# Transposing attention probabilities in 32-row pieces, four row groups into four banks, in a two-layer decoder kernel

## The reference

```python
scores = jnp.einsum('bhqd,bhkd->bhqk', Q, K) * scale
scores = jnp.where(mask == 0, jnp.float32(-1000000000.0), scores)
probs = jax.nn.softmax(scores, axis=-1)
attn = jnp.einsum('bhqk,bhkd->bhqd', probs, V)
```

## Time and profile before

| What | Value |
|---|---|
| Median of 3 runs | 1174.74 us (1174.51 to 1176.31) |
| The profiled execution | 1172.23 us, of which the span of the profile is 1170.4 us |
| Mean granted TensorE clock | 0.936 of full |
| PE / PEld busy | 946.8 us (81%) / 752.5 us (64%) |
| DVE / ACT / POOL busy | 888.7 us (76%) / 509.1 us (43%) / 309.4 us (26%) |
| One tile in the periodic stretch (l1 mixes start at 447.58 and 512.45 us) | 64.9 us |

### The profile page before, as it was taken

One profiled execution on the slowest core, in us unless ns is written; L12 is line 12 of the kernel. 1 busy time (PEld: TensorE's weight loads), 2 busy tenths in 40 slices (PEclk: granted clock), 3 DMA queues, 4 the chain that ended last, 5 costly groups with the idle time before them and its releaser, 6 DMA issues.

```text
span 1170.4 us, 23205 instructions
## 1 busy us (share of the span) xinstructions
PE 946.8 (81%) x8774; PEld 752.5 (64%) x8774; DVE 888.7 (76%) x2135; ACT 509.1 (43%) x1377; POOL 309.4 (26%) x508
## 2 busy tenths in 40 slices
PE   5657778888888888888888888888888888878754
PEld 5444656676676776776767766767666767657633
DVE  3775677888797888788797888878887888777452
ACT  2322436363536355363636354453636263534320
POOL 2561121312222222223222232232222222312121
PEclk9677999999999999999999999999999999989876
DMA  9102000000000000000000000000000000000000
GB/s 338 37 5 73 10 8 15 3 19 8 20 8 15 10 17 10 14 14 3 20 7 15 13 15 11 16 11 3 24 3 20 3 6 8 6 6 6 6 4 5
DMA packets 24414, 24.47 MB, mean 21 GB/s; under 512 B 2305, under 2 KB 22641, under 8 KB 24177
## 3 DMA queue, kind: packets, MB, share of 16 engines
q1 hardware_dynamic: 24304, 22.98, 6.1%
HBM read 18.80 MB, written 2.10 MB: 18 GB/s over the span
## 4 chain that ended last, share of the span: by engine, by line
DVE 47%; PE 30%; ACT 11%; issue 6%; POOL 6%; DMA 0%; DVEq 0%; POOLq 0%; SPq 0%
PE bank L1125 21%; PE bank L1240 9%; DVE peak L918 7%; ACT prob L663 6%; ACT prob L657 3%; DVE ma_ L1037 3%; DVE stats L847 2%; DVE q_top L809 2%; DVE y_ L861 2%; POOL scratch L528 2%; POOL rstd L522 2%; DVE k_ L1061 2%; DVE scratch L905 2%; DVE x_ L873 1%; DVE k_ L1070 1%
## 5 line engine op out<-in xcount | busy, mean ns | idle before, releaser
L663 ACT ACTIVATE prob<-bank,low 128x128 f32<-128x128 f32 x384 | 104.4, 382 | 156.6 <-DVE low L925 156.6
L1240 PE MATMUL bank<-cst,prob 128*128 128x128 f32 x768 | 117.2, 303 | 54.7 <-DVE y_ L861 39.0
L519 POOL TENSOR_TENSOR var_eps<-mean_var,rsq 128x1 f32<-128x1 f32 x144 | 28.4, 198 | 468.3 <-DVE mean_var L850 468.3
L1240 PEld LDWEIGHTS bank<-cst,prob 128*128 128x128 f32 x768 | 96.1, 156 | 71.9 <-issue 62.6
L918 DVE TENSOR_REDUCE peak<-bank 128x4 f32<-128x512 f32 x192 | 126.3, 684 | 20.8 <-PE bank L1125 20.8
L601 ACT ACTIVATE xt_<-bank 128x256 f32<-128x256 f32 x144 | 54.9, 393 | 130.5 <-PE bank L1240 130.3
L601 ACT ACTIVATE probT<-bank 128x512 f32<-128x512 f32 x192 | 103.5, 602 | 17.4 <-PE bank L1240 17.4
L522 POOL TENSOR_TENSOR rstd<-var_eps,rsq 128x1 f32<-128x1 f32 x144 | 79.8, 554 | 11.3
L1125 PE MATMUL bank<-w_gu,xt_ 128*128 128x352 f32 x256 | 81.0, 470 | 1.5 <-ACT w_f L601 1.0
L1125 PE MATMUL bank<-xt_,w 128*128 128x128 f32 x512 | 70.5, 304 | 0.5 <-ACT xt_ L601 0.5
L1125 PEld LDWEIGHTS bank<-xt_,w 128*128 128x128 f32 x512 | 69.4, 221 | 1.2 <-ACT xt_ L601 1.2
(11 more groups left out here) (180 smaller groups left out, 2202.7 us busy)
## 6 DMA issues: line engine op xcount, KB each, us to landing
xtin<-in_xT SPq DMA_DIRECT2D x16, 128.0 KB, 2.3
next_<-in_x SPq DMA_DIRECT2D x16, 128.0 KB, 6.9
ct_<-in_ctxT SPq DMA_DIRECT2D x16, 128.0 KB, 7.7
w<-in_w SPq DMA_DIRECT2D x2, 1024.0 KB, 6.1
out<-x_ SPq DMA_DIRECT2D x16, 128.0 KB, 1.7
next_<-x_ SPq DMA_DIRECT2D x16, 127.0 KB
rowt<-in_rows SPq DMA_DIRECT2D x1, 1664.0 KB, 7.7
w<-in_gate_up SPq DMA_DIRECT2D x2, 512.0 KB, 9.4
```

Of the source, the lines that this page charges most:

```text
L663: ins = act.activation(prob[:, r, c * P:(c + 1) * P], bank[r][:, c * P:(c + 1) * P], ACT.Exp, scale=SCALES[layer], bias=low[:, b, h:h + 1])
L1240: ins = pe.transpose(dst[:, k * P:(k + 1) * P], src[:, k * P:(k + 1) * P], ident)
```

## The change

`mix` now cuts each 128x128 transpose into four pieces of 32 queries. Piece g takes partitions 32g to 32g+31 of `prob` as the stationary operand (32 rows, 128 columns) and the 32x32 corner of the identity as the moving one (32 columns); it uses row group g of the array and writes 32 columns of bank `t{g}`. One mix is 64 such pieces. The bank no longer stands for the head group r but for the queries g, so each of the four banks is full only after the last r. TensorE waits for all four banks ahead of the first piece. ACT's four copies stay as many and as large; `value` reads the moving operand as four runs of 32 columns, 512 apart.

```diff
@@ STAGE_FILLS
-    ... _l + "_mix": [f"t{r}" for r in BANK_ORDER], ...
+    ... _l + "_mix": [f"t{g}" for g in range(4)], ...
@@ mix on ACT
-                    for r in BANK_ORDER:
-                        copy(i, (layer + "_mix", b, f"t{r}"), probT[:, r, :])
+                    for g in range(4):
+                        copy(i, (layer + "_mix", b, f"t{g}"), probT[:, g, :])
@@ mix on TensorE
                 def f(i, b):
+                    keys = [(layer + "_mix", b, f"t{g}") for g in range(4)]
                     for r in BANK_ORDER:
-                        key = (layer + "_mix", b, f"t{r}")
                         if r < 2:
                             pe.wait_ge(exped, at(i, SCORES, layer + "_scores", b, 2, r))
                         else:
                             wait_empty(pe, i, (layer + "_scores", b, S_BANKS[r]))
-                        turn_tile(i, key, prob[:, r, :], 4)
+                        if r == BANK_ORDER[0]:
+                            dsts = [free(i, key) for key in keys]
+                        for c in range(4):
+                            at0 = 32 * (4 * r + c)
+                            for g in range(4):
+                                part = slice(32 * g, 32 * g + 32)
+                                ins = pe.transpose(dsts[g][:, at0:at0 + 32], prob[part, r, c * P:(c + 1) * P],
+                                                   ident[part, part])
+                                if (r, c) == (BANK_ORDER[3], 3):
+                                    filled(ins, keys[g])
@@ weigh, value
-                        ins = mm(..., values[:, 4 * c + r, :], weights[:, r, c * P:(c + 1) * P])
+                        ins = mm(..., values[:, 4 * c + r, :], weights(r, c))
+            def turned(r, c):
+                at0 = 32 * (4 * r + c)
+                return probT[:, :, at0:at0 + 32]
-                    filled(weigh(dst, v_[:, b, :, :], probT), key)
+                    filled(weigh(dst, v_[:, b, :, :], turned), key)
```

More of the change, by code:

```diff
@@ L90 @@
 for _l in ("l0", "l1", "x1"):
-    STAGE_FILLS.update({_l + "_scores": S_BANKS, _l + "_mix": [f"t{r}" for r in BANK_ORDER], _l + "_value": ["y"],
+    STAGE_FILLS.update({_l + "_scores": S_BANKS, _l + "_mix": [f"t{g}" for g in range(4)], _l + "_value": ["y"],
                         _l + "_back": ["yb"], _l + "_turn": ["yt"], _l + "_out": ["o"]})
@@ L1314, in weigh @@
                     for r in range(4):
-                        ins = mm(dst[32 * r:32 * r + 32, c * P:(c + 1) * P], values[:, 4 * c + r, :],
-                                 weights[:, r, c * P:(c + 1) * P])
-                return ins
+                        ins = mm(dst[32 * r:32 * r + 32, c * P:(c + 1) * P], values[:, 4 * c + r, :], weights(r, c))
+                return ins
+            def turned(r, c):
+                at0 = 32 * (4 * r + c)
+                return probT[:, :, at0:at0 + 32]
             def value(layer):
@@ L1441, in l1_ma_value @@
                 dst = free(i, key)
-                filled(weigh(dst, e_[:, b % 2, :, :], ma_), key)
+                filled(weigh(dst, e_[:, b % 2, :, :], lambda r, c: ma_[:, r, c * P:(c + 1) * P]), key)
             def l1_ma_back(i, b):
```

## The result

| | Median, us | Ratio to before, 95% interval | Granted clock | At half clock, us |
|---|---|---|---|---|
| Before | 1175.53 | | 0.936 | 150 |
| Changed | 1269.68 (1267.76 to 1274.33) | 1.0806 (1.0774 to 1.0838) | 0.874 | 319 |

The change costs 94 us, where 41 had been forecast. The sign and the places were right; the time lies outside of the range, whose top was 1254. The last column is worked out as 2 x (1 - granted clock) x span, since the clock stood at one or the other of its two levels, 2.4 and 1.2 GHz, all the time.

A forecast was written before the change was run, and what follows sets the result against it. Bound by a chain of waits between engines through three mixes. 34 us (fifteen periods) + 3 (other mixes) + 4 (clock) = 41 on 1172.23, 1213; the median stands 2.5 higher: 1216 us. Range 1195 to 1235; 8 in 10: 1190 to 1254.

The forecast's parts named there:

- What bounds the kernel: No engine is full; a chain of waits passes through all three mixes of a period, and VectorE passes delays on in full.
- The pieces: In each mix, a round of four pieces takes 0.068 us, set by the load; 16 rounds take 1.09 us at full clock.
- rival 1: Slow loads in the mixes: 0.107 us a round, 75 us in all, 1250 us; chance 0.15.
- The banks: Mixes await four empty banks and hand over only at the end: next stage +0.61 to +0.77 (l0), +0.48 (x1), +1.05 us (l1).
- the terms for the waits and the pieces: Three mixes add 2.2 us a period, 34 us over fifteen periods, plus 3 us for the three mixes outside them.
- The late copies ahead of `l1_value`: Behind the l1 mix, all four copies end at about 516.6 in place of 515.15, delaying `l1_value`; costed at nothing.
- `value`: Its 16 matmuls stay; reading the moving operand in runs of 32 columns costs 0, upper end some 3 us.
- The clock: A few more l0 mixes fall to half clock, 1.7 us each: 4 us, with ends 0 and 12.
- Rival 2: The x1 or l1 mix also goes to half clock, 1.7 us a period: 25 us on top, 1241 us; chance 0.14.

The follow-up runs named there:

- the 64-row pieces: Kernel before, with the last two head groups of each mix transposed in 64-row pieces, two row groups into the two last banks; 1180.4 us.
- fillers ahead and behind: Changed kernel plus matmuls of constants, read by nobody, in TensorE's waits ahead of the pieces (11, 8, 2) and behind them (2, 0, 2); 1205.0 us.
- all its fillers: Kernel before plus matmuls of constants, read by nobody, in TensorE's waits in the mixes and in `x1_turn_h` (8 there); 1151.5 us.
- fillers in the mixes of the kernel before: Kernel before plus matmuls of constants, read by nobody, in TensorE's waits in the l0 and x1 mixes, none in `x1_turn_h`; 1167.5 us.

## Why the prediction was wrong

- *What bounds the kernel*: right. All three mixes were on the chain, and each delay went on in full.
- *The pieces*: right, slightly high. 64 pieces in 1.19 us are (1.19 - 0.22) / 63 x 4 = 0.062 us a round, against 0.068. The row groups load and multiply at once; loads of 32 rows x 128 columns of transposes cost 0.06 a round, not the 0.107 of rival 1. That the load sets this pace is borne out by the 64-row pieces: a round of two took 0.065 us, with twice the moving columns and half the instructions.
- *The banks*: right. From the last piece's start to the next stage 0.95 us in the l1 mix (559.01 to 559.96), against 0.97; the delays 0.66, 0.41 and 0.94 against 0.77, 0.48 and 1.05. With the mixes' waits filled on both sides, changed against before is 1205.0 - 1167.5 = 37.5 us, where the terms for the waits and the pieces were 34 + 3. That it fits so closely is in part luck, as the two weren't at half clock for the same time (127 and 137 us).
- *The late copies ahead of `l1_value`*: a small miss, costed at 0 ("so I add nothing for it"). A period without a fall of the clock shows it, first in the changed kernel with fillers ahead and behind (1205.0 us), then in the kernel before with all its fillers (1151.5 us):

```profile
530.36 0.42 DVE L975 TENSOR_TENSOR scratch<-bank,cst 128x256 f32<-128x256 f32 x1 [1.03 <-PE bank L1127]
...
534.28 1.08 PE L1127 MATMUL bank<-probT,v_ 128*32 128x128 f32 x32 [0.30 <-ACT probT L603]
...
542.28 2.48 DVE L1039 TENSOR_TENSOR ma_<-bank,cst 128x512 f32<-128x512 f32 x4 [0.18 <-PE bank L1127]
...
596.02 0.42 DVE L975 TENSOR_TENSOR scratch<-bank,cst 128x256 f32<-128x256 f32 x1 [1.04 <-PE bank L1127]
```

```profile
506.58 0.42 DVE L974 TENSOR_TENSOR scratch<-bank,cst 128x256 f32<-128x256 f32 x1 [1.04 <-PE bank L1126]
...
517.20 2.48 DVE L1038 TENSOR_TENSOR ma_<-bank,cst 128x512 f32<-128x512 f32 x4
...
569.65 0.42 DVE L974 TENSOR_TENSOR scratch<-bank,cst 128x256 f32<-128x256 f32 x1 [1.03 <-PE bank L1126]
```

  One tile takes 596.02 - 530.36 = 65.66 us and 569.65 - 506.58 = 63.07, so with the clock held the change costs 2.6 us a period. DVE's instructions behind the three mixes are later by 1.03 (l1), 0.81 (l0) and 0.46 us (x1), within 0.04 of the forecast 1.05, 0.77 and 0.48. The remaining 0.27 comes in at `ma_`: TensorE waits 0.30 us for the copies ahead of `l1_value`, and `ma_`, some stages on, now waits for TensorE. That is 4 us in all.
- *`value`* with its operand in runs of 32: the 32 instructions take 1.08 us before and after; costing it at 0 held.
- *The clock*: the step that failed. "I add 4 us for a few more that fall; the ends are 0 and 7 x 1.7 = 12." The fillers in the mixes give back 1269.7 - 1205.0 = 65 us in the changed kernel and 1175 - 1167.5 = 8 before, 57 us net. That 57 + 37.5 makes the 94 measured proves nothing, since the same four times stand in both; but the length of a period gives the same without them. It was 70.65 us on average in the changed kernel (DVE's `x0_project` at 273.27 and, 11 periods on, at 1050.46) and 64.8 before (253.42 and 1031.31, 12 periods), 5.8 more. Of these 2.6 are the banks with the clock held, and the 3.2 left are the clock: 48 us in 15 periods, and the ends beside them. I had limited it to the l0 mix, where the trace of before showed it, and to periods that had not fallen yet; it also fell at the x1 mix, in the waits for the copies and oftener at `x1_turn_h`, nearly three times a period in all. Rival 2 named the mechanism, but for one of the two mixes, at 25 us, and with a chance of 0.14. That one idle stretch of 2.2 of 4 us had stood at 1.00 was weak evidence against it: of two like waits in the l0 mix, the same trace showed one with a fall and one without. The range had no room for it to happen at several places at once. So the step that failed is the size and the reach of the clock term: about 57 us where it had 4, at most 12.

How a fall is tied to the idle time in detail stays open: the same wait of 2.80 us at the l0 mix is followed by half clock within the pieces in some periods, in `w_dn` in others, and why falls at `x1_turn_h`, to which the change does nothing, went from 5 to 10 I haven't settled; the wait there had grown from 2.2 to 3.1 us in seven of the ten. Its length alone isn't the reason: with fillers in the mixes of the kernel before it stayed at 2.2 to 2.3 us, and the falls went from 5 to 12.

## What to carry to other kernels

Splitting a transpose over the row groups does speed it up: 1.19 us here where it had been 1.91. But each row group fills a bank of its own, so no bank is full before the end, and the hand-over to the next engine changes from a pipeline of four to one block; look at when each bank is awaited and released before counting TensorE's own time. Where a change turns several short waits of TensorE into one long wait, price the clock at every such place, and not only where it has fallen before: here that was about 57 of 94 us. Holding the clock at one place can move its falls to the next, as the fillers in the mixes of the kernel before did; look at all places again after each step. Where TensorE waits for others anyway, idle matmuls into a free bank hold its clock, and were worth 2% in the kernel before; more of them cost 5 us again.

## What the runs showed of the hardware

Float32 transposes keep TensorE at full clock like matmuls: 1203.2 and 1205.0 us with either as fillers, both at a granted clock of 0.947. Float32 transposes of 32 rows x 128 columns keep a pace of 0.062 us for four row groups together, 0.0154 us a piece, 64 of them in 1.19 us; those of 64 rows keep 0.065 us for two row groups together, and full ones take 0.11 each. In the one mix that was read, a change from full to 64-row transposes cost 0.09 us (0.20 from start to start in place of 0.11), and the way back to a full matmul 0.04 (0.15 in place of 0.11). One fall of the clock cost 1.4 us at `x1_turn_h` (64.5 and 63.1 us a period).
